# Order of the work where attention ends and the expert tiles begin, in a decoder layer on one core

## What is computed

```
x = x + gated_recurrence(layernorm(x))                # stage A
x = x + cross_attention(layernorm(x), ctx)            # stage B: 16 heads, 77 keys, causal
x = x + moe(layernorm(x))                             # stage C: 4 experts, the best 2 of each row
moe: s = xf @ gate_W + gate_b; top 2; w = softmax of the two scores
     h = relu(layernorm(xf @ W1[e] + b1[e]) * g1[e] + be1[e])
     y = layernorm(h @ W2[e] + b2[e]) * g2[e] + be2[e];  out = sum_k w_k * y_k + xf
```

## Time and profile before

| | us |
|---|---|
| median of 3 runs (lowest, highest) | 1214.87 (1213.1, 1216.1) |
| the profiled execution, its own time | 1209.59 |
| its span | 1207.8 |
| PE busy (share of the span) | 1159.6 (96%) |
| DVE, ACT, POOL busy | 924.9, 731.5, 457.2 |
| mean granted TensorE clock | 0.988 of full speed |

### The profile page before, as it was taken

How to read it: one execution, slowest core, us unless ns; L and a number is a source line. 1 busy time by engine, 2 the same in 40 slices (tenths; PEclk the granted TensorE clock), 3 DMA queues, 4 the chain that set the end, 5 groups by cost and what they waited for, 6 DMA issues and landing times.

```text
span 1207.8 us, 24523 instructions
## 1 busy us (share of the span) xinstructions
PE 1159.6 (96%) x6041; PEld 978.9 (81%) x6042; DVE 924.9 (77%) x2196; ACT 731.5 (61%) x2114; POOL 457.2 (38%) x410
## 2 busy tenths in 40 slices
PE   6999999999989999999999998989999999999993
PEld 5788888888878888888888877867888888888882
DVE  6888888887766677877868777678777777777774
ACT  5323333233486757767677662567777777777773
POOL 4040000000052314535445164357655555555543
PEclk9999999999999999999999998899999999999998
DMA  8754544444520302133021358885554444444433
GB/s 271 230 160 160 188 176 146 174 156 165 199 84 1 105 10 97 44 107 104 10 97 44 131 131 227 270 221 122 81 88 81 85 79 86 80 85 80 85 64 42
DMA packets 83237, 143.90 MB, mean 119 GB/s; under 512 B 20460, under 2 KB 24752, under 8 KB 82309
## 3 DMA queue, kind: packets, MB, share of 16 engines
q1 hardware_dynamic: 63872, 101.60, 25.8%
q0 software_dynamic: 18464, 39.14, 17.1%
q10 hardware_dynamic: 837, 2.41, 0.6%
HBM read 78.83 MB, written 67.83 MB: 121 GB/s over the span
## 4 chain that ended last, share of the span: by engine, by line
PE 83%; DMA 5%; DVE 4%; issue 3%; ACT 3%; POOL 2%; POOLq 0%; DVEq 0%; SPq 0%; ACTq 0%
PE banks L1097 27%; PE banks L681 21%; PE banks L746 7%; PE banks L891 6%; PE banks L879 5%; DMA out<-rows,scatter_rows 4%; PE banks L848 3%; PE banks L865 3%; PE banks L1109 2%; PE banks L907 2%; PE banks L1125 2%; ACT rows L1310 2%; PE banks L719 1%; PE banks L800 1%; PE banks L765 1%
## 5 line engine op out<-in xcount | busy, mean ns | idle before, releaser
L1097 PE MATMUL banks<-operands 128*128 x1608 | 388.6, 396 | 10.5 <-DVE operands L1570 5.2
L1097 PEld LDWEIGHTS banks<-operands 128*128 128x128 f32 x1608 | 298.1, 189 | 73.6 <-issue 7.4
L681 PE MATMUL banks<-operands 128*128 128x512 f32 (+2 forms) x1224 | 292.6, 394 | 3.5 <-DVE operands L1570 3.5
L681 PEld LDWEIGHTS banks<-operands 128*128 128x128 f32 (+1 forms) x1224 | 225.6, 192 | 47.8 <-DVE operands L1570 3.7
L1570 DVE TENSOR_TENSOR operands<-banks,operands 128x512 fp32r<-128x512 f32 (+3 forms) x328 | 217.7, 682 | 42.5 <-ACT operands L1189 38.8
L1189 ACT ACTIVATE operands<-banks 128x512 fp32r<-128x512 f32 (+3 forms) x328 | 191.7, 608 | 96.7 <-PE banks L879 45.0
L1310 ACT ACTIVATE rows<-banks,score_shift 128x77 f32<-128x77 f32 x512 | 162.7, 374 | 28.0 <-DVE score_shift L1792 27.2
L1189 ACT ACTIVATE operands<-rows 128x512 fp32r<-128x512 f32 (+3 forms) x79 | 55.3, 709 | 163.8 <-DVE rows L1641 138.1
L1495 ACT ACTIVATE banks<-banks,param_cols 128x128 f32<-128x128 f32 x268 | 99.2, 430 | 82.5 <-PE banks L1125 82.5
L2576 POOL DMA_INDIRECT out<-rows,scatter_rows x67 | 106.6, 1591 | 104.2 <-DVE rows L2315 65.1
L1310 ACT ACTIVATION_READ_ACCUMULATOR rows<-banks,score_shift 128x1 f32 x512 | 129.1, 256 | 0.0
(11 more groups left out here) (178 smaller groups left out, 1707.0 us busy)
## 6 DMA issues: line engine op xcount, KB each, us to landing
expert_parts<-operands SPq DMA_DIRECT2D x32, 512.0 KB, 3.0
operands<-expert_parts SPq DMA_DIRECT2D x8, 2048.0 KB, 11.1
rows<-in_x SPq DMA_DIRECT2D x8, 1024.0 KB, 5.4
rows<-in_L_ffn_W SPq DMA_DIRECT2D x32, 256.0 KB, 3.5
x_rows<-rows SPq DMA_DIRECT2D x8, 1024.0 KB, 4.3
rows<-x_rows SPq DMA_DIRECT2D x8, 1024.0 KB, 5.7
xf_rows<-rows SPq DMA_DIRECT2D x32, 256.0 KB, 2.7
out<-rows SPq DMA_DIRECT2D x32, 256.0 KB, 2.5
```

Of the source, the lines that this page charges most:

```text
L681: last = nc.tensor.matmul(dst, stationary(a, k), moving(b, k), start=(t == 0 and k == 0), stop=(t == len(terms) - 1 and k == n_k - 1))
L1097: last = nc.tensor.matmul(dst, stationary[:, a, k, :], weights[:, w, bass.ds(e, 1), a2, k, :].rearrange("p e f -> p (e f)"), start=False, ...
```

## The change

It changes the order of work, and no product, norm or transfer is added or left out.

- **Last turn, DVE.** `plan_early(1)` (eight small instructions) moves from ahead of x2_rows(6, tile 0) to behind `read_positions`. `gate_bias` and `choose` of chunk 6 move from the end of the last turn to behind the first x2_rows of the last chunk.
- **Gates of chunk 6, PE.** The gate products of the first tile stay at the end of the last turn; those of tiles 1, 2 and 3 are put between the halves of the first projection, behind it, and into first_product(0).
- **First products.** first_product(0) comes behind the first projection instead of behind all four and the positions; first_product(1) behind the third. Both banks are primed in the last turn, and ACT fills both banks at its start (before: `route_weights` and six base rows stood around them).
- **Tail of the last chunk.** The transposes of xf tiles 2 and 3 and rows_in for tile 3 move from in front of tile 0 to its end. The gate products move from tile 0 into tile 1 (two tiles' worth in first_product(3), two in second_product(1)), the positions into tile 2. DVE's `choose` goes to tile 1, `count` to its end, and all later steps of the route and the plan go one tile later.
- **ACT, tile 0.** hidden_norm(1) now stands ahead of the wait for the stored xf rows; rows_hi(3) still stands behind it. POOL's rstd(-1), the root for tile 0, moves ahead of half of the scatters and of both ln3_pow of the last chunk; SP's `expert_in(1)` ahead of the stores of the last chunk's xf rows. Two of the product banks are swapped.

The core of the diff:

```diff
-        cx_bank, m1_bank, m2_bank = (... for pair in ((4, 5), (6, 3), (1, 7)))
+        cx_bank, m1_bank, m2_bank = (... for pair in ((4, 5), (6, 7), (3, 1)))
+        tail_g_bank, tail_r_bank = cx_bank[1], cx_bank[0]
...
@@ SP
+            expert_in(1)
             sp.wait_ge(mm_done, mm_num(NCH, "o3") + 1)
             for j in range(TPC):
                 store_xf(last, j)
             for i in range(2):
                 sp.wait_ge(base_out[i], 16 * 2 * last)
             load_rows(g2_rows, "L0_ffn_g2", g2_in)
-            expert_in(1)
...
@@ PE, last_turn
-                prime(m1_bank[0])
+                for bank in m1_bank:
+                    prime(bank)
                 rows_in(0, 1)
-                gate_scores(c)
+                gate_scores(tail, (0,))
...
@@ PE, c_tile
+                if early == 0:
+                    pe.wait_ge(mm_read, mm_num(tail, "o3") + 1)
                 if after >= 2:
                     hidden_in(i, u)
-                if after >= 3:
+                if early == 0:
+                    pe.wait_ge(mm_read, mm_num(tail, "r") + 1)
+                    prime(m2_bank[0])
+                if early == 2:
+                    pe.wait_ge(tail_gate_read, 1)
+                if early == 3:
+                    pe.wait_ge(tail_pos_read, 1)
+                if after >= 3 and early >= 1:
                     rows_in(n + 1 + u, 1 - u)
-                if early == 0:
-                    pe.wait_ge(b_t_read, t_num(tail, "xf3") + 1)
-                    prime(m2_bank[0])
-                    gate_products(tail_bank, tail, range(TPC)).then_inc(tail_gate_done, 1)
...
-                    first_product(i + 2, u, experts[4])
-                second_product(i, u, experts[2], (i + 1, 1 - u) if 1 <= after < 3 else None)
+                    first_product(i + 2, u, experts[4], prime_and_gates if early == 1 else
+                                  last_positions if early == 2 else None)
+                second_product(i, u, experts[2], last_gates if early == 1 else
+                               (lambda: hidden_in(i + 1, 1 - u)) if 1 <= after < 3 else None)
                 if early == 0:
-                    pe.wait_ge(tail_gate_read, 1)
-                    pe.wait_ge(route, NROUTE * last + ROUTE_COUNTED)
-                    position_products(tail_bank, True).then_inc(tail_pos_done, 1)
+                    for j in range(2, TPC):
+                        xf_to_features(last_of_b, tail, j)
+                    rows_in(1, 1)
...
@@ PE, behind last_turn
-            for j in range(TPC):
-                project(last, tail, j)
-            positions(last - 1, tail, "r")
-            pe.wait_ge(plan_ready, 1)
-            first_product(0, 0, expert_at(pe, 0))
-            for j in range(2):
-                xf_to_features(last, tail, j)
-            pe.wait_ge(mm_read, mm_num(tail, "o3") + 1)
-            prime(m1_bank[1])
-            first_product(1, 1, expert_at(pe, 1))
-            for j in range(2, TPC):
-                xf_to_features(last, tail, j)
-            rows_in(1, 0)
+            pe.wait_ge(plan_ready, 1)
+            project(last, tail, 0, (0, 1))
+            gate_scores(tail, (1,))
+            project(last, tail, 0, (2, 3))
+            first_experts = [expert_at(pe, 0)]
+            gate_scores(tail, (2,))
+            first_product(0, 0, first_experts[0], lambda: gate_scores(tail, (3,)))
+            project(last, tail, 1)
+            project(last, tail, 2)
+            first_product(1, 1, first_experts[1])
+            project(last, tail, 3)
+            rows_in(1, 0)
+            positions(last - 1, tail, "r")
+            for j in range(2):
+                xf_to_features(last, tail, j)
...
@@ ACT, c_tile
+                if after >= 1:
+                    hidden_norm(i + 1, 1 - u)
                 if early == 0:
                     act.wait_ge(b_t_done, t_num(NCH, "xf3") + 1)
                     for j in range(TPC):
                         act.wait_ge(xf_out[j], 16 * NCH)
                     act.dma_start(be2_rows, ...).then_inc(be2_in, 16)
...
                 if after >= 3:
                     rows_hi(i + 3, 1 - u)
+                if early == 1:
+                    act.wait_ge(be2_in, 16)
+                    act.wait_ge(b_t_read, t_num(NCH, "xf3") + 1)
+                    weighed_be2(0, 0, experts[1])
...
@@ DVE, c_tile
                 hidden_lo(i)
-                if early == 0:
+                if early == 1:
                     dve.wait_ge(tail_gate_done, 1)
-                    biased_scores(tail_bank).then_inc(tail_gate_read, 1)
+                    biased_scores(tail_g_bank).then_inc(tail_gate_read, 1)
                     choose(NCH - 1, None)
-                    count(NCH - 1)
-                if early >= 1:
+                if early == 2:
+                    dve.wait_ge(tail_pos_done, 1)
+                    shifted_positions(tail_r_bank, True).then_inc(tail_pos_read, 1)
+                if early >= 2:
                     out_rows(*last)
                 if after >= 2:
                     statistics(i + 2, 0, m1_bank[u], m1_done, c1_stat)
                     moments(i + 2, 0, c1_stat, c1_aggr)
+                if early == 0:
+                    for j in range(2, TPC):
+                        xf_features(NCH - 1, NCH, j)
+                    coming()
                 if after >= 3:
                     rows_lo(i + 3, 1 - u)
+                if early == 1:
+                    count(NCH - 1)
+                    out_rows(*last)
...
@@ DVE, behind last_turn
             x2_rows(last, tail, 0)
+            gate_bias(tail)
+            choose(last - 1, tail)
+            statistics(0, 0, m1_bank[0], m1_done, c1_stat)
+            moments(0, 0, c1_stat, c1_aggr)
+            add_eps(-1, True, False)
+            rows_lo(1, 1)
             count(last - 1)
+            norm_shift(0)
             x2_rows(last, tail, 1)
             ln3_pair(last, 0)
             weigh(last - 1)
             x2_rows(last, tail, 2)
             for j in range(2):
                 ln3_apply(last, tail, j)
+            statistics(1, 0, m1_bank[1], m1_done, c1_stat)
+            moments(1, 0, c1_stat, c1_aggr)
             x2_rows(last, tail, 3)
...
```

138 lines of the change are left out of this document (69 added, 69 removed).

## The result

The changed kernel takes 1221.11 us (median of 10 runs, 1217.73 to 1223.9), the kernel before 1216.9 in the same comparison (10 runs, 1213.1 to 1219.67). The ratio of the two, over all the runs, is 1.0046, with a 95% interval of 1.0029 to 1.0062. That is 5.6 of 1216.9 (the medians alone are 4.2 apart). The forecast was no change, 1213.9, with 1218.5 as the upper end, so it was wrong in sign and size. Of the 7.2 between 1213.9 and 1221.11, 2.0 come from the kernel before, whose median is 1216.9 here and was 1214.87 in the three runs on which the forecast was built. The profiled execution has a span of 1220.9 and a time of 1222.72, against 1207.8 and 1209.59 before, so the profile shows 13.1 more. I come back to that gap.

The account below looks back on a forecast made before the run. PE was taken as the bound, busy 96%. Gains of 12.6 against losses of 13.7 put tile 3 1.1 later; with -1.0 at the end, 1208.6 profiled became a forecast median of 1213.9, no change, range 1207.5 to 1218.5.

Parts of the forecast that it names:

- Item 7: Before first_product(3), PE waits for ACT, which waits for the last xf store: 6.0 lost, bounds 2 and 8.
- What comes behind: Tiles 3 to 8, output chain: the 1.1 delay at tile 3 shrinks to -1.0 to 0 by hidden_lo(7), then stays.
- items 1: Projections in the tail: the clock no longer falls during 48 projection products, 2.8 gained.
- 3 (the bias fill): Two waits go, 1.50 for tile 1's bias fill and 2.39 for tile 3's gathered rows: 3.9 gained.
- What would show it: Signs: no clock fall 721 to 740, PE idle 4 to 8 before first_product(3) released by ACT, clock fall near 760.
- Item 6: Tile 0: DVE reaches hidden_lo(0) later than PE, 2.5 lost, bounds 0 and 4.
- Item 8: The clock falls again while PE idles for the xf stores: 1.9 lost.
- Item 9: Tiles 1 and 2: PE waits for DVE, 1.0 for count and 2.3 for hidden_lo(2), 3.3 lost, bounds 1 and 5.
- Items 1 to 5: Gains up to tile 3 from clock, waits, plan_early(1) and small gaps: 12.6 together, unhindered PE starting tile 3 at about 768.
- items 1 to 3 and 5: Gains: clock in projections 2.8, clock in tile 0 and gates 2.9, two waits 3.9, small gaps 2.0.
- item 4: DVE's plan_early(1) no longer stands ahead of x2_rows, where PE waited: 1.0 gained, bounds 0 and 2.1.
- slower rival: First output DMA goes out after expert load 5, one more output meets a load: +4.2, 1219.1; slower had 0.15.

Follow-up runs that it names:

- x13: x6 with SP, not ACT, loading be2 behind expert load 2, and the remaining slot tables ahead of loads 5 to 7, issued back to back; ratio 1.0015.
- x15: x6 with SP, not ACT, loading be2, then load 2, ahead of load 3; experts 2 to 4 reported behind two slot tables, not eight; ratio 0.9958.
- x18: The changed kernel with experts 2, 3 and 4 reported by SP behind two slot tables instead of eight, nothing else; ratio 1.0033.
- x3: The changed kernel with SP's load of expert 3 moved behind the xf stores; ratio 1.0043.
- x5: The changed kernel with SP's order alone changed: all four base rows and g2 earlier, expert load 3 behind the xf stores; ratio 1.001.
- x6: x5 plus a changed DVE order in tile 1 and the positions one product later; ratio 1.0005.
- x10: The changed kernel with 50 products whose result nothing reads added on PE ahead of first_product(3); ratio 1.007.
- x11: x6 with 15 products whose result nothing reads added on PE ahead of first_product(3); ratio 1.0013.
- x2: The changed kernel, unedited, profiled a second time; span 1220.8, time 1222.56.
- x1: The kernel before, unedited, profiled a second time; span 1206.2, time 1208.04.
- x7: The kernel before with only plan_early(1) moved behind read_positions in DVE's last turn; ratio 0.9988.
- x17: The kernel before with experts 2, 3 and 4 reported by SP behind two slot tables instead of eight; ratio 0.9986.
- x14: The kernel before with expert loads 5 to 7 back to back and slot tables moved ahead of the reports of experts 2 to 4; ratio 1.0059.
- x4: The changed kernel with be2 loaded by SP behind the g2 rows, so SP instead of ACT waits for the xf stores; ratio 1.0035.
- x8: The kernel before with the SP order of x5; ratio 1.0007.
- x16: As x15, but with be2 asked for behind expert load 2 instead of ahead of it; ratio 0.9962.

## Why the prediction was wrong

In short, three steps failed. Item 7, the wait for the xf stores, was priced at 6.0 with 8 as its bound and measured 12.25 and 10.94 in the two profiles of after. It named one transfer where two ended the stretch. And "What comes behind" had a late tile 3 made up for, where the runs show that it is kept.

**Right: items 1, 3 (the bias fill) and the place of the loss.** PE reaches tile 1 at +32.2 in the profiles of the changed order (+32.9 in x13 and x15), the clock is 1.00 up to there, 24 projection products take 5.62. The wait stands before first_product(3), released by ACT for the stores, and the clock falls in it, as "What would show it" has it.

**Item 6 (2.5): the right engine in most profiles, and twice too high.** PE waited 1.41 in tile 0 of after, and what ended it there was SP's report of expert 1, behind the slow tables. In x18, as in x3, x5, x6, x10 and x11, it was 1.2 for DVE's hidden_lo(0), the wait that was forecast; tile 1 starts at +32.2 either way.

**Item 7 (6.0, bounds 2 and 8): the step that failed in size.** 12.25 in after and 10.94 in x2, but 5.46 in x18. The forecast took the landing as fixed by the bytes ("Their bytes queue behind the same 2.5 MB"). What it left out is ahead of them on SP: the four slot tables, whose length it took from one execution (726.48 to 742.44, 15.92), as part of the 742.44 of load 3. Most of that length is one wait of SP, until load 1 and the four stores ahead of the tables are through (last section). They took 19.63 and 18.56 in the two profiles with the long wait, and ACT issued be2 at +43.6 and +43.5; with 15.92 (x18) and 16.88 (x10) it was +36.7 and +36.3. My 758.5 is +37.0. The kernel before does the same: with tables of 15.9 to 17.5 (before, x1, x7, x17) be2 went out at +37.3 to +37.9, and with 20.53 (x14, whose edit stands behind all this) at +43.9. So the price of item 7 went with SP's tables, from 5.5 to 12.3, and the upper bound of 8 was too low. That it went with them is read from profiles side by side; no run sets the length of the tables, and whatever makes the bytes ahead of them slow could slow the xf stores as well. What it is stays open. Item 7 also missed the second transfer, g2, that ended the same stretch (x3, x4).

**Item 8 (1.9): right in x18 (2.0 for a wait of 5.46) and in x2 (1.9 for one of 10.94), three times too small in after (6.0 for 12.25).** The Trainium skill ("TensorE: Matmul & The Clock Gate", Why this matters for your kernels) warns of idle gaps between bursts; x10 against after agrees with it.

**Item 9 (3.3): 2.6 in after** (0.46 for count, 2.18 for hidden_lo(2)); x6, which takes most of it away, is 1.0005 against x5's 1.001.

**Items 1 to 5 (12.6): more than there was to give back, and sized on one execution.** Items 6 to 9 put tile 3 at 781.7, which is +60.2, and x18 has +60.5. That agreement is luck. In x18 the four items are 1.2, 5.5, 2.0 and 2.7, 11.3 together and not 13.7, so an unhindered PE would have been at +49.2 and not at the forecast's 768 (+46.5). x15 says much the same: PE was busy 48.3 of the 51.9 up to tile 3, at a clock of 1.00. The forecast's own count of PE's work was 47.9 of 58.75, so that only 10.9 were not work, and with the 0.4 between load 1 and 721.87 it gives the same +48.3. The sum took 11.6 from it with items 1 to 3 and 5, and 1.0 more with item 4, which moves load 1 as well.

The other side of the comparison did not come out either. I compared with +59.2, and four more profiles with the order of before (x1, x7, x8, x17) have +55.9, +56.1, +57.5 and +56.6. The 48 projection products took 12.5 to 13.3 in them against 13.92, and tile 0 was 12.6 to 14.9 long against 16.56. A fifth, x14, has +60.0 and a tile 0 of 17.7, because there the slow tables and the late stores held up the kernel before too. The kernel x14, timelines of SP and PE:

```profile
731.99 20.53 SPq L606 DMA_DIRECT2D rows<-slot_table  x4
```

```profile
771.63 1.12 PE L1125 MATMUL banks<-ident,rows 128*128 128x128 f32 x4 [2.73 <-ACT rows L1512]
```

None of the five has the 2.39 for gathered rows that I took "in full". The "+1.1 at tile 3" was thus 3.9 with short tables (x18 against x17) and 7.4 and 11.2 with long ones (x2 and after against x14).

**"What comes behind": failed in sign.** I had the difference shrink to between -1.0 and 0, "set by the end of load 7". It is 3.9 at tile 3 between x18 and x17 (+60.5, +56.6) and 6.9 from load 1 to the end of the span (490.5, 483.6). Between after and x1 it is 15.3 at tile 3 and 14.2 at tile 10. POOL's output DMAs are the chain: the first went out at 788.34 in after, 6 behind load 5 (782.43), where before had it 1.1 ahead of load 5. The kernel after, timeline of POOL:

```profile
788.34 1.63 POOL L2618 DMA_INDIRECT out<-rows,scatter_rows  x1 [15.69 <-DVE rows L2349]
794.16 1.60 POOL L2618 DMA_INDIRECT out<-rows,scatter_rows  x1 [0.91 <-DMA out<-rows,scatter_rows]
804.42 1.61 POOL L2618 DMA_INDIRECT out<-rows,scatter_rows  x1 [4.62 <-DMA out<-rows,scatter_rows]
```

That is the condition of the slower rival ("The late first output", over 2 later), and its 1219.1 was the nearer number. Its mechanism is only part of it: the wait comes first, and the chain passes it on. In these profiles a delay at tile 3 was still there at tile 10 (15.3 and 14.2 above), and a lead was not: x15's 4.0 over x1 was 0.5 at tile 10, and x11's 1.7 had turned into 3.1 behind. That a lead is lost in the output chain is read from these few profiles and was not tested by a run of its own.

**How much of the timed loss is settled.** SP's order, with both transfers early, takes 0.36 of the 0.46% back (x5, bounds 0.14 and 0.58) and does nothing for the kernel before (x8). With be2 off ACT and the report early the changed order is 0.4% faster than before. The early report alone explains neither (x17, x18). Three things stay open. The kernel before was never run with all of x15's or x16's order on SP and be2 off ACT together, and the intervals of x15 and x17 touch, so the share of the change in x15's gain isn't measured. What makes SP's tables long in some executions is not known. And how often they are long in timed executions isn't either: the gap between profiles and timed runs comes for the most part from quick profiled executions of before, and x18's profile is 6.9 above x17's where timed they are 0.47% (5.7) apart.

## What to carry to other kernels

Before pricing a wait, look at what its issuing queue does ahead of it, and profile the kernel before more than once: here a row of 15.92 that could be 19.6 or 20.5, and a wait of 2.39 present in one profile of six, went into the sum as constants. Compare the profiled execution's own time with the timed runs, too: it was shorter than all of them here. Where a stall is removed, ask which other transfer would end the same stretch; two behind one another must be moved together (x3, x4, then x5). And when work is pulled forward, the reports and loads behind which it will next stand have to be pulled forward with it: the changed kernel was 0.46% slower than before with the old order on SP and 0.4% faster with the transfers and the expert reports early.

## What the runs showed of the hardware

Each slot table is a load of 1 KB, and by the program SP issues one only when the one two before it has landed. The four behind load 1 took 14.6 to 20.5 over the profiles, apart from x8, and nearly all of it is one wait. The kernel after, timeline of SP in two windows:

```profile
728.43 1.63 SPq L608 DMA_DIRECT2D rows<-slot_table  x2
```

```profile
746.10 1.97 SPq L608 DMA_DIRECT2D rows<-slot_table  x2
```

The first two go out at once behind load 1 (2 MB) and four stores (1 MB), all on SP's queue. The third goes out 17.7 later, when the first has landed; load 1 itself had landed at +18.3 and the two xf stores behind it at +20.0 and +20.7. The other profiles have 13.2 to 18.9 for that wait. In x8 the tables are issued only at +17.9, when load 1 is through, and the same wait is 4.1. With no expert load under way six tables took 5.97 in x18:

```profile
781.27 5.97 SPq L608 DMA_DIRECT2D rows<-slot_table  x6
```

So a load of 1 KB costs 1 by itself here and 13 to 19 behind 3 to 3.5 MB on its queue, and what it costs there varied by 3.2 between executions of the same program up to that place (17.7 in after, 17.1 in x2, 14.5 in x18). The Trainium skill ("DMA: Bandwidth & Descriptors", Queues, rings and completion order) says that on each DMA engine descriptors are consumed in ring order, though a later one may finish its write first. These rows agree with the first part, and no run here shows the second.

After PE's idle of 12.25 the clock stayed at 1.2 GHz through 12.8 us in which the profile has PE busy all the time, and after 10.94, with the same products in the same order, through 3.8. The kernel after, windows from first_product(3) on, then the same in x2:

```profile
767.50:780.29 12.79, 12.79 (x39) 10.76 (x40) 2.99 (x10) 6.00 (x12) 2.73 (x3) 0.50 0.72 250
```

```profile
769.90:773.65 3.75, 3.73 (x9) 2.97 (x10) 3.00 (x10) 1.80 (x5) 1.53 (x2) 0.50 0.55 201
```

After 5.46 (x18) it was 4.1. What the clock costs after a wait does not follow from the length of the wait alone.

The clock also fell where PE had no wait. In all six profiles with the order of before it fell in the run of 32 gate products at the start of the tail, or right behind it (+3.2 to +4.7). In the fourteen of the changed order, where these products are spread, it did not fall before tile 1.
